# A hybrid block on one core: second feed-forward front in another order, and filler multiplies in the last attention unit

## What is computed

```python
def ffn(x):                                   # x: layer-normalised, 2048 x 128
    shared_out = (silu(x @ shared_gate_w) * (x @ shared_up_w)) @ shared_down_w
    logits = x @ gate_w                       # 2048 x 32
    topk_ids, topk_val = argmax(logits), max(logits)
    xs = x * sigmoid(topk_val)[:, None]
    order = argsort(topk_ids)                 # rows grouped by expert
    g, u = grouped_mm(xs[order], gate_w_of_expert), grouped_mm(xs[order], up_w_of_expert)
    d = grouped_mm(silu(g) * u, down_w_of_expert)
    return shared_out + d[argsort(order)]

x = x + attn_a(layernorm(x))
x = x + ffn(layernorm(x))
x = x + attn_b(layernorm(x))                  # q k^T in blocks of 16, exp, times v, divided by the sum of weights, w_out
x = x + ffn(layernorm(x))
```

## Time and profile before

| what | value |
|---|---|
| median of the runs of before | 559.16 us (557.72 to 559.17, 3 runs) |
| the profiled execution | 557.5 us, of which 555.6 us from the first to the last instruction |
| mean granted clock of TensorE | 0.979 of full |
| busy: PE, DVE, ACT, POOL | 495.6, 425.7, 291.0, 251.4 us |
| last attention unit to the first step of the expert loop | about 443 to 497 us of the span |

### The profile page before, as it was taken

One profiled execution on the slowest core, in us unless ns is written; L12 is line 12 of the kernel. 1 busy time (PEld: TensorE's weight loads), 2 busy tenths in 40 slices (PEclk: granted clock), 3 DMA queues, 4 the chain that ended last, 5 costly groups with the idle time before them and its releaser, 6 DMA issues.

```text
span 555.6 us, 16703 instructions
## 1 busy us (share of the span) xinstructions
PE 495.6 (89%) x6472; PEld 304.0 (55%) x6472; DVE 425.7 (77%) x979; ACT 291.0 (52%) x624; POOL 251.4 (45%) x294
## 2 busy tenths in 40 slices
PE   6989888897989997999999999999999868989991
PEld 3323232355444443777767777777767655544540
DVE  3386968988747766868899888899878988847762
ACT  3544344254448864666545555446644433448870
POOL 3556777555514545253344443333233435633542
PEclk9999999999999999999999999999999988999996
DMA  6799920000269862100000000000000000169964
GB/s 183 313 425 283 99 21 0 2 0 20 76 190 268 271 216 72 30 4 21 21 21 22 22 22 22 22 21 21 22 21 8 7 2 11 42 187 275 276 217 139
DMA packets 45326, 54.11 MB, mean 97 GB/s; under 512 B 10880, under 2 KB 36416, under 8 KB 44224
## 3 DMA queue, kind: packets, MB, share of 16 engines
q1 hardware_dynamic: 42688, 47.78, 29.6%
q0 software_dynamic: 2560, 5.26, 2.7%
HBM read 43.55 MB, written 9.48 MB: 95 GB/s over the span
## 4 chain that ended last, share of the span: by engine, by line
PE 59%; DVE 24%; issue 6%; DMA 4%; POOL 3%; ACT 2%; DVEq 0%; SPq 0%; POOLq 0%; ACTq 0%
PE psum L1249 9%; PE psum L1730 7%; PE psum L1748 7%; PE psum L1823 5%; PE psum L1802 4%; PE psum L1268 4%; PE psum L1256 3%; DVE arena L761 3%; POOL sorted_x L1467 2%; PE psum L1771 2%; DVE arena L755 2%; PE psum L277 2%; PE psum L278 2%; DVE arena L2032 2%; DVE arena L2027 2%
## 5 line engine op out<-in xcount | busy, mean ns | idle before, releaser
L2202 POOL TENSOR_TENSOR arena<-arena 128x512 f32<-128x512 f32 x32 | 40.9, 1297 | 110.2 <-issue 103.0
L1495 POOL DMA_INDIRECT y_tok<-arena,to x48 | 46.6, 971 | 64.8 <-ACT arena L1318 63.4
L1918 ACT ACTIVATE arena<-psum 128x512 f32<-128x512 f32 x64 | 37.9, 597 | 45.2 <-PE psum L1730 42.0
L1730 PE MATMUL psum<-arena 128*128 128x512 f32 x128 | 59.2, 605 | 0.8 <-ACT arena L1901 0.7
L1249 PE MATMUL psum<-experts,arena 128*32 x96 | 50.2, 604 | 1.1 <-ACT arena L1308 1.1
L1249 PE MATMUL psum<-arena 128*32 128x512 f32 x288 | 50.9, 605 | 0.0
L661 POOL TENSOR_TENSOR arena<-arena 128x512 f32<-128x512 f32 x32 | 37.2, 1181 | 26.2 <-DVE arena L761 17.5
L1748 PE MATMUL psum<-arena 128*128 128x128 f32 x384 | 47.5, 278 | 1.4 <-ACT arena L1923 1.4
L1748 PEld LDWEIGHTS psum<-arena 128*128 128x128 f32 x384 | 45.2, 191 | 2.4 <-ACT arena L1923 2.4
L2139 POOL TENSOR_TENSOR arena<-arena 128x256 f32<-128x256 f32 (+4 forms) x75 | 33.9, 452 | 24.5 <-ACT arena L1937 17.9
L1730 PEld LDWEIGHTS psum<-arena 128*128 128x128 f32 x128 | 22.9, 189 | 35.6 <-issue 34.0
(11 more groups left out here) (240 smaller groups left out, 1204.1 us busy)
## 6 DMA issues: line engine op xcount, KB each, us to landing
arena<-in_experts SPq DMA_DIRECT2D x48, 384.0 KB, 4.4
experts<-in_experts SPq DMA_DIRECT2D x8, 1536.0 KB, 17.4
arena<-sorted_x SPq DMA_DIRECT2D x48, 64.5 KB, 3.8
sorted_x<-zeros SPq DMA_DIRECT2D x2, 1536.0 KB, 13.4
arena<-in_w_qkv SPq DMA_DIRECT2D x16, 192.0 KB, 3.4
arena<-y_tok SPq DMA_DIRECT2D x8, 256.0 KB, 3.1
x_tok<-in_x SPq DMA_DIRECT2D x4, 256.0 KB, 4.9
arena<-in_w_out SPq DMA_DIRECT2D x16, 64.0 KB, 1.9
```

What stands on the lines that cost most here:

```text
L1495: pool.indirect_dma_start(out=y_tok, out_offset=bass.IndirectOffsetOnAxis(ap=f_to[:, s:s + 1], axis=0), in_=f_gy[(s + 4) % 8], in_offset=N ...
L1730: pe.matmul(ring("in", n, j)[:, :], b_w[n % 2][:, which * P:which * P + P], x, start=True, stop=True)\
L1918: act.activation((b_q, b_k)[which][:, part * CHUNK:part * CHUNK + CHUNK], src, ACT.Copy, scale=(D_B ** -0.5, 1.0)[which]).then_inc(h["drai ...
L2202: pool.tensor_tensor(b_yn[:, part], b_y[:, part], b_rec[:, part], ALU.mult).then_inc(h["normed"], 1)
```

## The change

In the last attention unit PE gets five products whose results nobody reads (three ahead of the ROUGH scores, two behind them), DVE instead of POOL multiplies the second half of the last unit, and half of the shared expert's first chunk moves ahead of the last `project_out`. In the second front (k = 1; the first front keeps its order) `first_slots` moves behind the statistics, chunk 3 is normalised ahead of `first_rows`, logits of chunk 2 go ahead of the transposes of chunk 3, `second_places` is cut in two, and shared work moves behind the routing. Two keep-clock products go for k = 1.

```diff
@@ second_places is cut
             row_numbers(dve, chain, a, 1)
+
+        def slot_experts(dve, chain, k):
+            before, a = half_of(k, 0), half_of(k, 1)
             chain(dve.tensor_scalar(before.cmp[:, 0:EXPERTS], before.taken, place_col[:, 1:2], None, ALU.is_le))
...
@@ f_pe, k == 1
             else:
                 front_turn(pe, k, 2)
+                front_logits(pe, k, 2)
                 front_turn(pe, k, 3)
-                front_logits(pe, k, 2)
                 front_logits(pe, k, 3)
+                shared_half(pe, k, 1, 0, 1)
+            count_tokens(pe, k, 1)
+            if k == 0:
+                shared_half(pe, k, 1, 0, 1)
+            else:
                 shared_out(pe, k, 0)
-            count_tokens(pe, k, 1)
-            shared_half(pe, k, 1, 0, 1)
             shared_half(pe, k, 1, 1, 2)
-            keep_clock(2)
+            if k == 0:
+                keep_clock(2)
             shared_half(pe, k, 2, 0)
+            if k == 1:
+                shared_out(pe, k, 1)
             done(pe, "slot_col", 1)
             pe.matmul(bank[7][0:1, 0:P], f_slot_col, ident, start=True, stop=True).then_inc(t["slot_row"], 1)
-            shared_out(pe, k, 1)
+            if k == 0:
+                shared_out(pe, k, 1)
@@ f_act, k == 1
                 gate_shared(act, k, 0, 0)
+                gate_shared(act, k, 0, 1)
                 front_norm(act, k, 2)
-                gate_shared(act, k, 0, 1)
@@ f_dve
                 row_ids(dve, k)
-                first_rows(dve, chain, k)
...
             ins.then_inc(t["xn_last"], 1)
             if k == 1:
+                first_rows(dve, chain, k)
+                route(dve, chain, k, 2, 2)
+                product_shared(dve, k, 0, 1)
+                second_places(dve, chain, k)
+                add_shared(dve, k, 0)
                 for n in range(2):
-                    product_shared(dve, k, 0, n)
-                route(dve, chain, k, 2, 2)
+                    product_shared(dve, k, 1, n)
+                slot_experts(dve, chain, k)
@@ b_pe
+            def fill_wait(cols):
+                for at in range(0, cols, CHUNK // 2):
+                    pe.matmul(ring("out", LAST - 1, 0)[:, 0:CHUNK // 2], ident, const[:, 0:CHUNK // 2], start=True, stop=True)
...
+                        if n == LAST and i:
+                            pe.wait_ge(h["normed_late"], 1)
...
+                if n == LAST:
+                    pe.wait_ge(h["acc"], 2 * (LAST - 1))
+                    fill_wait(CHUNK + CHUNK // 2)
                 if now:
                     scores(n, ROUGH)
+                if n == LAST:
+                    fill_wait(CHUNK)
...
                 else:
+                    pe.wait_ge(h["y_out"], UNITS)
+                    shared_half(pe, 1, 0, 0)
                     project_out(n - 1)
-                    pe.wait_ge(h["y_out"], UNITS)
-                    for half in range(2):
-                        shared_half(pe, 1, 0, half)
+                    shared_half(pe, 1, 0, 1)
@@ b_dve
+            def normalise_late():
+                part = slice(CHUNK, SEQ)
+                dve.wait_ge(h["y_out"], UNITS)
+                dve.wait_ge(h["o"], 2 * LAST)
+                dve.tensor_tensor(b_yn[:, part], b_y[:, part], b_rec[:, part], ALU.mult).then_inc(h["normed_late"], 1)
...
                 if n == UNITS:
-                    first_slots(dve, chain, 1)
+                    normalise_late()
+                    product_shared(dve, 1, 0, 0)
...
+            first_slots(dve, chain, 1)
             dve.wait_ge(h["acc"], 2 * LAST)
@@ b_pool_engine
-                for j in range(2):
+                for j in range(2 if n < LAST else 1):
```

More of the change, by code:

```diff
@@ L51 @@
 FOUND = 4
-SLOT_BOUND = "second_places keeps the expert of a slot between 0 and EXPERTS - 1"
+SLOT_BOUND = "slot_experts keeps the expert of a slot between 0 and EXPERTS - 1"
 ROW = C + 1
@@ L1374, in f_dve @@
                 route(dve, chain, k, 3, 1)
-            add_shared(dve, k, 0)
-            second_places(dve, chain, k)
-            for n in range(2):
-                product_shared(dve, k, 1, n)
+                add_shared(dve, k, 0)
+                second_places(dve, chain, k)
+                slot_experts(dve, chain, k)
+                for n in range(2):
+                    product_shared(dve, k, 1, n)
             done(dve, "slot_row", 1)
@@ L1593, in hybrid_block @@
             "shift xn xt x pooled packed packed_odd ready coarse proj drained scored subbed turned expd weighed merged summed y_out z_out divided normed o biased "
-            "acc logits_in").split()}
+            "acc logits_in normed_late").split()}
         w_in, wo_in, bias_in = [sem(f"b_w_in{r}") for r in range(2)], [sem(f"b_wo_in{r}") for r in range(2)], sem("b_bias_in")
@@ L1819, in project_out @@
                     if i % 4 == 0:
-                        pe.wait_ge(h["normed"], 2 * n + i // 4 + 1)
+                        if n == LAST and i:
+                            pe.wait_ge(h["normed_late"], 1)
+                        else:
+                            pe.wait_ge(h["normed"], 2 * n + i // 4 + 1)
                         if n < LAST:
```

## The result

The change makes the kernel slower: 561.0 us against 558.5 (medians of 22 runs each), a ratio of 1.0042 with a 95% interval of 1.0026 to 1.0059. The prediction was 558.8 us, no change that a measurement can tell, and 560.6 at the upper end of its range.

What follows compares the result with a forecast made beforehand. Bound: the expert loop on PE, its start set by the last scatter's landing. Addition -2.5, first scatter +0.5, ninth -1.3, weights take back 0.9 at the landing: -0.4, so 558.8 us from 559.16; range 556.9 to 560.6.

Steps and rivals of the forecast that it cites:

- the price of the low clock in the routing: PE's transposes and logits before `route`: 1.2 GHz expected, costing 1.5 us, so `route` starts at 470.7 instead of 469.2.
- the landing: Last scatter, issued 3.75 behind SP's first weights, lands 3.95 after issue, at 493.4; the weights take back 0.9.
- The fillers: Five unread products in PE's waits of the last attention unit: cost nothing, hold the clock, sums done 1.5 earlier.
- The late half of the product: Last unit's second half multiplied on DVE: 0.69, at most 1.4 if POOL holds it up; costs nothing.
- The first addition: DVE's addition behind the last `project_out`: starts at 458.85 instead of 461.35, 2.5 earlier; 1.25 earlier if fillers do nothing.
- the first scatter: POOL's first early scatter: at 469.35, 0.5 later than before, since 3.0 of DVE work is put in between.
- That last term: `first_slots` on DVE: 1.9 at its new place instead of 3.40, nothing added for `front_power` beside it; by the rule up to 1.25 more.
- Slot list: From what the second `placed` releases on POOL to SP's weights issue: 3.0 before, 2.1 more net now; issue at 485.75 at low clock.
- nothing in the change touches: Expert loop, 24 PE steps behind 497 us: unchanged by the edit, so only when the loop can start counts.
- Rival 2: Fillers don't hold the clock and weights go out later into the scatters: +0.9 to +1.9, 560.1 to 561.1; chance 0.18.
- Rival 1: PE stays at 2.4 GHz through the routing: -1.3 to -1.8, 557.9 to 557.4; chance 0.27.
- Rival 3: Nothing moves: landing or PE's shared work stays, or `front_power` holds up `first_slots` by 1.25; 0, 559.2; chance 0.10.

Runs made afterwards that it cites:

- fillers in the routing: After with slot list built early, shared half ahead of the first transposes, and four unread 128x256 products in the routing's waits: 555.62 us, ratio 0.9953 to before.
- half of the weights: After, with SP sending the weights of slots 2 and 3 only behind the second and third read of slots: 560.31 us, ratio 1.0036 to before.
- the list early: After, with `slot_experts` right behind `second_places` and the list turned ahead of `shared_out(1)`: 558.69 us, ratio 1.0003 to before.
- a shared half early: After with slot list built early and `shared_half` of chunk 1 moved from behind the logits to ahead of the first transposes: 556.03 us, ratio 0.9968 to before.

## Why the prediction was wrong

Three steps of it failed: the price of the low clock in the routing, the landing, and the loop's first steps, which the sum had at nothing.

**Held.** The fillers keep the clock (1.00 from 444 to 466) and the sums are done 1.46 earlier; 1.5 was said. (Against three other executions without fillers it is 0.5 to 0.7, against a fourth 1.5, so a part of the agreement is the luck of before's profiled execution.) The late half of the product took 1.32 on DVE, at most 1.4 was said, and PE asked for it later. The first addition has a shift of -2.54 (said -2.5), the first scatter +0.39 (said +0.5), `first_slots` takes 1.90 (said 1.9).

That last term had a choice in it. In after, L1107 (both inputs in SBUF) ran from 464.45 to 465.13 beside `front_power` (464.63 to 465.94) and took 0.68, what the prediction had read for the scan of this size alone. The Trainium skill, SBUF — State Buffer, Who interferes with whom, would have the two exclude each other for their whole length; no row of DVE shows it here, as L1116 had not before. (POOL's row took 1.31, the `front_power` before it 1.02; which of the two was held up, if any, no run shows.) Taking the row and not the rule was right.

**Routing: the price of the low clock, 1.5.** The price was too small. From the addition to `route` it is 12.46 in after; with the clock held (fillers in the routing) it is 10.35, just what the prediction counted for full clock. So the low clock costs 2.1 in this execution (1.3 in that of "half of the weights", with the same order on PE). Between `route` and the ninth scatter another 0.4 was lost (10.38, before 9.96), in small pieces of `second_places`, such as L1092 at 0.40 instead of 0.19. The ninth scatter gained 0.27 where 1.27 was predicted: this step is short by 1.0.

**Slot list: 2.1 net.** It measured 1.7: from the ninth scatter to SP's weights 4.69, before 3.00. Together with the ninth scatter the weights shift by 1.42, where 0.83 was predicted.

**Landing: 3.95.** It measured 4.93, 1.0 too little again. I interpolated between scatters of before that stood 3.3 and 4.6 behind the first weight, but these were single transfers in the middle of a row of others. With the list early the scatter before the last stood just 4.14 behind the first weight and landed after 3.8; the last one of after, at the same 4.14, took 4.93. Some 0.6 of this 1.1 is the packet that came out as an instruction packet ended, of which no row of before gave a sign; the rest is open. That the weights would take back some of the gain was right; 0.9 was said, and they took 1.9.

These two steps of 1.0 make the difference at the slots' reading: -0.4 was predicted, +1.6 measured.

**Missing: "nothing in the change touches" the loop.** This sentence of the first part failed. The prediction counted PE's shared work as early enough and stopped there. But it ended 2.33 before slot 0 was there, where before it ended 0.20 before that, and behind this idle the first two steps ran at 0.50 to 0.64: +1.4, nearly half of the shift of 3.1. The prediction had read both low stretches of before as coming right behind idle PE, and did not apply that to the place where its own sum made PE idle.

**The rivals.** Rival 2's deciding point ("as soon as the ninth starts after 481.0") is what happened: at before's anchor the ninth starts at 481.65 and the last scatter lands at 495.4, inside its 494.7 to 495.75. Its condition was wrong: it had tied this to fillers that fail, and the fillers held while the routing took their gain back. Its chance was too low for that reason. Rival 1 did not happen in after (logits of 1.9); the version with fillers in the routing makes it happen, that with a shared half early for the first logits at least, and with the list early these are faster than before by 0.5% and 0.3%. Rival 3 is refuted at both its parts: the landing moved, and `front_power` held up nothing.

## What to carry to other kernels

When one chain gets faster, look at what else starts on its way: here a list that was late by 1.4 us sent a bulk transfer into the last small transfers that the next stage waits for, and this cost more than the chain had gained. Put what issues bulk DMA early on every queue that it passes (here six short DVE instructions and one on PE), and work that nobody waits for behind it. And where a sum makes TensorE wait ahead of a stage that it bounds, count the first steps of that stage at the low clock too, or put work into the wait (tried here once: the time was better, 559.17, but its profile does not show that the clock held).

## What the runs showed of the hardware that was not expected

- One packet can hold up a scatter's landing when the DMA engines are all but idle. With half of the weights held back the DMA share was 0.15 in 492 to 494 and 0.02 from 494 on, and the last scatter still landed 4.28 after its issue: one of its packets started at 493.84, as an instruction packet of 1.39 ended (493.86), while the others were through by 492.54. In after the same is seen with an instruction packet of 1.02, for 0.6.
- The clock stayed low through a stretch in which PE was hardly idle: in after it stood at 0.50 in 468 to 470, with PE busy 1.96 of 2.00 in logits and transposes, and the rows show 1.00 again only behind the shared half that follows (0.83 in 476 to 478, 1.00 from 478).
- A little work in the routing's waits moved much. With a shared half of two products ahead of the transposes `route` came 1.4 nearer to the anchor than with the early list alone (0.5 nearer than in "half of the weights", the best execution without it), with four products of 128x256 (about 0.5 each, 1.03 for the first two) another 0.8.
